# First chunk of a graph attention layer: one mask indicator and a third product in place of a second indicator

## The reference

```
Wh = layernorm(x) @ W.T + b
e[i,j,h] = leaky_relu(src[i,h] + dst[j,h], slope 0.2)
att = softmax over j of (e where adj[i,j] == 1, else -9e15)
x[i] = x[i] + sum over j of att[i,j,h] * Wh[j,h,:]
```

## Time and profile before

| | us |
|---|---|
| median of 3 executions | 759.43 |
| lowest and highest | 757.79, 763.54 |
| span of the profiled execution | 758.4 |
| mean granted TensorE clock | 0.905 |

### The profile page before, as it was taken

The page is one execution under the profiler, slowest core; times in us unless marked ns, Lnnn a source line. Parts: engine busy times, 40 slices in busy tenths (PEclk is TensorE's granted clock), DMA queues, the critical chain, the costliest instruction groups (busy, mean ns, idle before and its releaser), DMA issues.

```text
span 758.4 us, 14829 instructions
## 1 busy us (share of the span) xinstructions
PE 623.6 (82%) x5288; PEld 471.8 (62%) x5288; DVE 532.9 (70%) x1050; ACT 388.6 (51%) x761; POOL 209.0 (28%) x151
## 2 busy tenths in 40 slices
PE   2446566799999999989999969995469969979696
PEld 2435555587776877758777655775446737747453
DVE  3379999966677757867577189458597998997300
ACT  3382579577786687747878536541013213222231
POOL 3339908011111211112101120714600801702100
PEclk9985899599999999989999989998669979969889
DMA  9603363001111011110111110101264735726744
GB/s 187 120 1 57 57 168 56 1 2 57 57 56 56 24 34 57 57 58 7 51 57 56 57 55 1 56 1 46 75 202 134 218 107 160 230 69 178 224 117 119
DMA packets 30702, 63.08 MB, mean 83 GB/s; under 512 B 4556, under 2 KB 7636, under 8 KB 30644
## 3 DMA queue, kind: packets, MB, share of 16 engines
q1 hardware_dynamic: 28020, 52.83, 23.7%
q0 software_dynamic: 2624, 9.44, 6.2%
HBM read 69.59 MB, written 1.05 MB: 93 GB/s over the span
## 4 chain that ended last, share of the span: by engine, by line
PE 63%; DVE 18%; ACT 7%; issue 5%; DMA 3%; POOL 3%; SPq 2%; DVEq 0%; ACTq 0%; POOLq 0%
PE bank L608 16%; PE bank L620 12%; PE bank L568 9%; PE bank L692 6%; PE bank L553 4%; PE bank L729 4%; PE bank L722 3%; DMA att<-in_gb 3%; DVE arena L1219 3%; DVE arena L1207 2%; ACT arena L965 2%; POOL reg_b L465 2%; DVE reg_c L1361 2%; DVE arena L1215 2%; ACT ysb L926 1%
## 5 line engine op out<-in xcount | busy, mean ns | idle before, releaser
L965 ACT ACTIVATE arena<-sbc,nd 128x512 bf16<-128x512 f32 x204 | 130.5, 719 | 34.7 <-PE bank L568 34.7
L458 POOL TENSOR_TENSOR x<-x,ysb 128x512 f32<-128x512 f32 x36 | 62.2, 1728 | 309.2 <-ACT ysb L926 304.9
L568 PE MATMUL bank<-reg_b,arena 128*128 128x99 bf16 x2048 | 106.6, 217 | 20.6 <-DVE arena L1219 15.6
L608 PE MATMUL bank<-hTc,arena 128*128 128x512 f32 x256 | 121.4, 630 | 0.0
L620 PEld LDWEIGHTS bank<-arena,reg_c 128*128 128x128 f32 x1024 | 116.8, 192 | 7.2 <-issue 7.2
L568 PEld LDWEIGHTS bank<-reg_b,arena 128*128 128x128 bf16 x2048 | 103.6, 103 | 24.8 <-DVE arena L1219 13.7
L620 PE MATMUL bank<-arena,reg_c 128*128 128x128 f32 x1024 | 116.9, 275 | 0.0
L916 ACT ACTIVATE reg_c<-bank,b 128x512 f32<-128x512 f32 x128 | 87.9, 688 | 36.8 <-PE bank L608 36.8
L1207 DVE TENSOR_TENSOR arena<-maskT,arena 128x2048 bf16<-128x2048 bf16 x48 | 67.7, 1411 | 48.2 <-ACT arena L965 48.0
L1219 DVE TENSOR_TENSOR arena<-maskT,arena 128x2048 bf16<-128x2048 bf16 x64 | 95.2, 1488 | 2.2
L1361 DVE SCALAR_TENSOR_TENSOR reg_c<-reg_b,nd,reg_c 128x512 f32<-128x512 f32 x144 | 96.4, 744 | 0.0
(11 more groups left out here) (170 smaller groups left out, 772.1 us busy)
## 6 DMA issues: line engine op xcount, KB each, us to landing
arena<-in_wrT SPq DMA_DIRECT2D x128, 256.0 KB, 3.1
reg_c<-in_adj POOLq DMA_DIRECT2D x16, 512.0 KB, 8.4
arena<-in_w1T SPq DMA_DIRECT2D x16, 512.0 KB, 3.9
arena<-in_w2T SPq DMA_DIRECT2D x16, 512.0 KB, 4.8
x<-in_x SPq DMA_DIRECT2D x4, 256.0 KB, 3.6
out_x<-x POOLq DMA_DIRECT2D x4, 256.0 KB, 3.9
arena<-in_wsT SPq DMA_DIRECT2D x1, 512.0 KB, 3.8
arena<-in_gW SPq DMA_DIRECT2D x2, 64.0 KB, 8.2
```

What stands on the lines that cost most here:

```text
L458: nc.gpsimd.tensor_tensor(xi, xi, ysb[:, e % 3, :].rearrange("p (t d) -> p t d", d=P), ALU.add).then_inc(s_acc, 1)
L568: last = mm(bank[i // 2][:, o:o + VW], ind[:, q, b, j, i * P:(i + 1) * P], u[:, (t * H + h) * 2 + b, :, :], start=(t == 0 and i % 2 == 0 a ...
L608: mm(bank[b][:, :], w1[:, s, e % 2, c * P:(c + 1) * P], hTc[:, :], start=True, stop=True).then_inc(full[b], 1)
L965: last = af(ind[:, q, 1, j, :], sbc[:, h, :], ACT.Relu, bias=nd[:, q * QT + j, h:h + 1], scale=BIG)
```

## The change

Only chunk 0 of the first attention layer. DVE no longer makes the second selecting matrix there. With M the mask's tile and A the first indicator, PE now runs three products where it ran two: A with the values of sign 0 (as before), A with the negated values of sign 1, and M with the values of sign 1; the last two add up in the PSUM columns that held the second sum. The negated values are made on DVE by one TENSOR_SCALAR per head (`negate`, 16 tiles of 99 columns, bf16), and lie where the second indicator of one quad lay. `attend_first(h)` waits for them (`s_neg`) ahead of all its quads, and DVE issues `negate(h)` behind all four quads of `select_first(h)` for heads 1 to 3, and behind `split` for head 0. ACT's scaled logits of chunk 0 go to side 0 of `ind`, where DVE takes the minimum in place. The other chunks go on as before; `s_g` counts from chunk 1.

```
+        ind1 = arena[:, 0:8192].bitcast(BF16).rearrange("p (q x) -> p q x", q=Q)
+        negu = ind1[:, :, QT * CW:QT * CW + T * VW].rearrange("p h (t w) -> p h t w", t=T)
...
+        s_neg = sem("negated_values_ready")
...
+            def attend_first(h):
+
+                use(0, "att")
+                use(1, "att")
+                pe.wait_ge(s_neg, h + 1)
+                for q in range(Q):
+
+                    pe.wait_ge(s_ind, k.event("ind"))
+                    for j in range(QT):
+                        t = q * QT + j
+                        for i in range(CT):
+                            o = (i % 2) * 2 * VW
+                            sel = ind[:, q, 0, j, i * P:(i + 1) * P]
+                            mm(bank[i // 2][:, o:o + VW], sel, u[:, (t * H + h) * 2, :, :],
+                               start=(t == 0 and i % 2 == 0), stop=(t == T - 1), skip_group_check=True)
+                            mm(bank[i // 2][:, o + VW:o + 2 * VW], sel, negu[:, h, t, :],
+                               start=False, stop=False, skip_group_check=True)
+                            last = mm(bank[i // 2][:, o + VW:o + 2 * VW], maskT[:, t, i * P:(i + 1) * P],
+                                      u[:, (t * H + h) * 2 + 1, :, :],
+                                      start=False, stop=(t == T - 1), skip_group_check=True)
+                            if t == T - 1 and i % 2:
+                                last.then_inc(full[i // 2], 1)
+                    if q < Q - 1:
+                        last.then_inc(s_indf, 1)
...
             for h in range(H):
 
                 pe.wait_ge(s_u, h + 1)
-                attend(h)
+                attend_first(h)
...
+                side = 0 if isinstance(n, int) and n < H else 1
                 for j in range(QT):
-                    last = af(ind[:, q, 1, j, :], sbc[:, h, :], ACT.Relu, bias=nd[:, q * QT + j, h:h + 1],
+                    last = af(ind[:, q, side, j, :], sbc[:, h, :], ACT.Relu, bias=nd[:, q * QT + j, h:h + 1],
                               scale=BIG)
...
+            def select_first(h, quads=range(Q)):
+
+                for q in quads:
+                    if q:
+
+                        dve.wait_ge(s_above, h * (Q - 1) + q)
+                        last = v.tensor_tensor(ind[:, q, 0, :, :], maskT[:, q * QT:(q + 1) * QT, 0:CW],
+                                               ind[:, q, 0, :, :], ALU.min)
+                    else:
+                        dve.wait_ge(ev["rows"], h + 1)
+                        if h:
+
+                            dve.wait_ge(s_indf, (h - 1) * (Q - 1) + 1)
+                        for t in range(QT):
+                            last = v.scalar_tensor_tensor(ind[:, 0, 0, t, :], sbc[:, h, :], thr[:, t, h:h + 1],
+                                                          maskT[:, t, 0:CW], ALU.is_gt, ALU.mult)
+                    last.then_inc(s_ind, 1)
+
+            def negate(h):
+
+                dve.wait_ge(s_u, h + 1)
+                v.tensor_scalar(negu[:, h, :, :].rearrange("p t (s v) -> p t s v", v=V1), u6[:, :, h, 1, :, :], -1.0,
+                                None, ALU.mult).then_inc(s_neg, 1)
...
-                        if not (isinstance(n, int) and n == 0):
-
-                            dve.wait_ge(s_indf, (n - 1) * (Q - 1) + 1)
+                        dve.wait_ge(s_indf, (n - 1) * (Q - 1) + 1)
...
-                    dve.wait_ge(s_g, n * Q + (q + 1))
+                    dve.wait_ge(s_g, (n - H) * Q + (q + 1))
...
             dve.wait_ge(ev["mask"], 2 * CT)
-            indicate(0, 0, range(1))
+            select_first(0, range(1))
             dve.wait_ge(s_exp, 1)
             split(v, 0, then)
+            negate(0)
...
             for h in range(H):
-                indicate(0, h, range(0 if h else 1, Q))
+                select_first(h, range(0 if h else 1, Q))
+                if h:
+                    negate(h)
                 if h == 1:
 
                     dve.wait_ge(s_xb, C)
```

## The result

The changed kernel takes 771.45 us (median of 4 executions, 767.39 to 772.26) where the kernel before takes 758.61; the ratio is 1.0163, 95% interval 1.0119 to 1.0207. It is slower, by 12.4 us at that ratio (the two medians lie 12.8 apart). The forecast was 771, in a range of 762 to 778.

The account below looks back on a forecast made before the run. DVE was taken to bound the first chunk; the wait, products and negation made head 3 end 12.0 us later, the tail -0.5, so +11.5: span 758.4 to 769.9, plus 1.0 to the median, forecast 771 us, range 762 to 778.

Parts of the forecast that it names:

- The wait serialises the engines: First chunk: the negation stands behind quad 3, so PE, ACT and DVE run one after the other; +11.5 us in sum.
- The stretch on ACT: From a head's last product to the end of the next head's quad 3 logits: 11.1, 10.0 and 11.05 us.
- Minimum and negation: On DVE behind the last logits: minimum 1.2, negation 1.0, hand-over 0.1, 2.3 us; 2.7 for heads 1 and 3.
- What would show it: Signs in the changed profile, among them heads 1 to 3 starting 11 to 14 us behind the previous head's last product.
- if the negation takes over 2 us: Sign that the prediction is wrong: DVE's negation, taken as 1.0 us between 0.47 and 1.9, lasting over 2 us.
- 192 products: PE's attend of each first-chunk head: 10.5 us with 1.6 lost to the clock; ends 8.9 and 13, sign 9 to 11.
- Head ends: Last products of heads 0 to 3 in the first chunk at 67.5, 91.8, 114.6 and 138.85 us.
- The tail: From head 3's last product to ACT's copy of the normalised chunk: the copy follows ACT's list, -0.5 us.
- Around the span, and behind the chunk: Profiled span 758.4 taken as 1.0 us under the median; the first chunk's delay shifts all the rest whole.
- Rival 1: First chunk: wait there but small, longer bursts keep PE's clock high, negation cheap at 0.47; 762.5 us, within 1%; chance 0.12.
- Rival 2: First chunk: negation done before PE has transposed its rows, so the wait doesn't hold PE; 755.5 us; chance 0.07.
- Rivals 3 and 4: 3: rival 2 with rival 1's clock, about 750 us, 0.04; 4: split values or row transposes wait elsewhere, 776, 0.05.

Follow-up runs that it names:

- the early negation: Changed kernel with the negation of heads 1 to 3 issued behind quad 0 of its head, no longer behind quad 3: 752.45 us, 0.9921 to the kernel before.
- the extra product: Kernel before plus a third product in the first chunk, 192 products a head, with its two indicators, order and waits kept: 758.66 us, ratio 0.9999.

## Why the prediction was right, point by point

**The wait serialises the engines: right, and it costs more than the whole loss.** The step "nothing of head h can start until it is done" is in the chain of waits after. The wait alone, put into the kernel before, costs as much as the change (1.0189, 1.0163). Moving the negation, with the same instructions, takes back all of it and 0.8% more: the wait costs 19 us, and without it the exchange of subtractions for products gains 6.

**The stretch on ACT: right.** 11.0, 10.1 and 11.0 us for 11.1, 10.0 and 11.05. That the late sums of head 1 would no longer be held by the merge held too.

**Minimum and negation: 1.4 us short in sum, the second mis-sized both ways.** From the last logits to the first product: 4.1, 2.0 and 3.0 us for 2.7, 2.3 and 2.7. So head 1 starts 15.1 us behind the last product of head 0, outside the 11 to 14 of "What would show it". The negation is 0.58 us alone, below my 1.0 and near my lower end of 0.47, and 2.65 beside GpSimd, above my upper end of 1.9. I had put 0.4 us on the turn of POOL and it was up to 2.1: in head 1 two instructions of GpSimd, from 79.43 to 81.54 us, lie within the negation's 79.35 to 82.00. By my own sign, "if the negation takes over 2 us", the prediction would be wrong here; it moves head 1 by 1 us and leaves the mechanism as it was. By the Trainium skill ("VectorE: DVE Perf Modes", the perf-mode tier table) the estimate was 0.6 us: the trace agrees, 0.58. By another rule of the Trainium skill ("SBUF — State Buffer", SBUF: two separate sides), that such a form and GpSimd lock the pair against each other for a whole instruction: the trace agrees, 0.58 us with GpSimd idle, and 1.34, 2.65 and 1.53 with it at work.

**192 products: right for heads 1 to 3.** 10.2, 10.9 and 10.4 us for 10.5 each; head 0 took 11.3, over the 9 to 11 foreseen. The range had room for only 0.85 us more in each, though I had kept 13 us an attend as its upper end; at that end the time would have been 781, above the range.

**Head ends: right, the first in part by luck.** 67.2, 92.4, 115.5 and 139.9 for 67.5, 91.8, 114.6 and 138.85. Head 0 started at 55.84 us, not 57.0, and took 0.8 us longer: two errors that cancel.

**The tail: wrong by 0.5 us.** I took 0.5 off since the copy would follow ACT's list; it came 12.35 us behind the last product (12.4 before). PE's transposes of the normalised chunk start at 151.03, once ACT has copied the last mask row out of their bank (150.89 in the chain). The list is not only ahead of the copy but ahead of what the copy needs.

**Around the span, and behind the chunk: errors that cancelled.** The span of the changed kernel lies 2.05 us under its execution's own time (769.2 and 771.25), and no execution on record has less than 1.85 between the two. So the profiled execution of the kernel before, with its span of 758.4, took about 760.5, not the median's 759.4. And the chunk ended 13.0 us later (139.26 to 152.24) where I had 11.5, but the stretch behind it shrank by 2.2; I had it pass the delay on whole. The second chunk's first attend starts 12.0 us later (153.74 and 165.76). That the forecast of 771 meets the 771.45 so closely is luck; the mechanism, borne out head by head above, is not.

**The rivals.** Rival 1 (clock high, negation cheap): the granted clock was 0.76 to 0.80 on average in each of the four windows, the attends took 1.3 to 2.4 us more than the 8.9 at the full clock, and the negation was cheap only where GpSimd was idle. Rival 2 (the wait doesn't hold) is not what the changed kernel does, but it is what the early negation does: 755.5 foreseen, 752.45 measured, with head 2 starting at 92.2 for about 93 and the head ends 0.9 to 2.3 us earlier than worked out. Rivals 3 and 4 did not come.

## What to carry to other kernels

Where a producer makes a matrix in pieces and a consumer starts on the first piece, whatever is added to the consumer's start must be ready as early as the first piece: placed behind the last one, a 0.6 us instruction cost 19 us, because the last piece needed the end of the turn before. Work taken from the engine that bounds a stretch is worth what the next engine leaves: here the exchange of VectorE's subtractions for TensorE's products pays while GpSimd makes VectorE dear (heads 0 and 1 together) and not afterwards (heads 2 and 3: 749.05 us without it, 752.45 with it, first chunk 93.0 and 96.2). By the medians head 0 alone has nearly all of the gain (750.58); that head 1 adds to it isn't shown. Before such a trade, ask of each new wait what the instruction ahead of the awaited one waits for itself.

## What the runs showed of the hardware that I had not expected

- VectorE's one-input bf16 TENSOR_SCALAR of 1584 elements a partition, rows of 99 elements that start at odd places, took 0.58 us, 0.37 ns an element, where the two-input subtraction of 2048 takes 1.22, 0.60 ns an element. No run has it in an even layout, so what the odd one costs isn't shown. Beside GpSimd it took up to 2.65 us, 2.1 of them with two GpSimd instructions running. A merge of seven small instructions takes 2.6 us with GpSimd idle and took 7.5 to 9.6 beside its split.
- The same instructions, behind first chunks of different lengths, took 613.6 to 619.7 us; one turn of 56.3 or 53.4 us went with a granted clock of 0.54 or 0.77 in its first 14.8 us. A change of 5 us in one place can so be hidden in the total, as the extra product was.
